# Layer 1's prototype bias as stacked half-precision parts instead of a full-precision product

## The reference

```
topw, topi = top_k(softmax(-dists / t), 2);  topw = topw / sum(topw)
out = zeros
for tslot in range(2):
    idx, wt = topi[:, tslot], topw[:, tslot:tslot + 1]
    h = einsum('nri,ni->nr', B[idx], xf)          # rank 16
    out = out + wt * (einsum('nor,nr->no', A[idx], h) + bias[idx])
x = x + tanh(g_ffn[1]) * out
```

## Time and profile before

| | us |
|---|---|
| median of 3 runs | 3636.69 (3634.04 to 3637.95) |
| profiled execution, its time | 3638.66 |
| profiled execution, its span | 3636.8 |
| PE busy, share of the span | 3096.3, 85% |
| DVE busy | 2824.3, 78% |
| ACT busy | 2012.7, 55% |
| POOL busy | 1970.1, 54% |

### The profile page before, as it was taken

How to read it: one execution, slowest core, us unless ns; L and a number is a source line. 1 busy time by engine, 2 the same in 40 slices (tenths; PEclk the granted TensorE clock), 3 DMA queues, 4 the chain that set the end, 5 groups by cost and what they waited for, 6 DMA issues and landing times. The chain is left out here.

```text
span 3636.8 us, 107677 instructions
## 1 busy us (share of the span) xinstructions
PE 3096.3 (85%) x35590; PEld 2626.8 (72%) x35590; DVE 2824.3 (78%) x6978; ACT 2012.7 (55%) x4103; POOL 1970.1 (54%) x3561
## 2 busy tenths in 40 slices
PE   4999884777777777599986999999999999999998
PEld 2666663565655656499984888888888888888886
DVE  5777775878788888656536988888888888888896
ACT  2666664777777777345533554545554555555553
POOL 0000004656566565000003888888888888888887
PEclk8999997999999999799997999999999999999999
DMA  3666562222222221211012232323232323232321
GB/s 118 264 265 246 234 254 58 74 71 64 73 71 64 73 71 53 89 48 47 23 36 87 76 99 87 100 87 100 88 99 87 100 87 100 87 100 87 100 86 52
DMA packets 352441, 364.00 MB, mean 100 GB/s; under 512 B 109953, under 2 KB 332673, under 8 KB 347137
## 3 DMA queue, kind: packets, MB, share of 16 engines
q1 hardware_dynamic: 338944, 333.23, 28.5%
q10 hardware_dynamic: 12960, 25.23, 1.9%
q0 software_dynamic: 160, 0.52, 0.1%
HBM read 213.11 MB, written 145.78 MB: 99 GB/s over the span
## 5 line engine op out<-in xcount | busy, mean ns | idle before, releaser
L365 POOL TENSOR_TENSOR a_probT_lo<-a_expT,a_probT_hi 128x512 f16<-128x512 f32 (+1 forms) x384 | 371.4, 995 | 343.2 <-ACT a_probT_hi L433 343.2
L933 POOL TENSOR_TENSOR a_pn<-a_prob,a_rsum 128x1232 f32<-128x1232 f32 x128 | 360.3, 2815 | 6.6 <-DVE a_rsum L1273 6.6
L1031 ACT ACTIVATE a_qT_hi<-banks 128x512 f16<-128x512 f32 x256 | 152.8, 597 | 360.2 <-PE banks L140 360.2
L138 PE MATMUL banks<-a_vo,a_probT_hi 128*128 128x256 f16 x1280 | 349.2, 273 | 2.7 <-DVE a_probT_lo L1246 2.6
L139 PE MATMUL banks<-a_vo,a_probT_hi 128*128 128x256 f16 x1280 | 349.2, 273 | 0.0
L140 PE MATMUL banks<-a_vo,a_probT_lo 128*128 128x256 f16 x1280 | 349.0, 273 | 0.0
L138 PE MATMUL banks<-a_xnT_hi,w_q_hi 128*128 128x256 f16 x1024 | 282.3, 276 | 4.7 <-DVE a_xnT_lo L1244 4.5
L139 PE MATMUL banks<-a_xnT_lo,w_q_hi 128*128 128x256 f16 x1024 | 282.3, 276 | 0.0
L140 PE MATMUL banks<-a_xnT_hi,w_q_lo 128*128 128x256 f16 x1024 | 282.2, 276 | 0.0
L424 ACT ACTIVATE a_expT<-banks,a_top,w_score_scale 128x512 f32<-128x512 f32 (+1 forms) x384 | 269.7, 703 | 22.6 <-PE banks L519 11.5
L1967 POOL PARTITION_ALL_REDUCE w_tops<-w_part_tops x1 | 0.4, 368 | 498.3 <-DVE w_part_tops L1994 498.3
(11 more groups left out here) (346 smaller groups left out, 12469.7 us busy)
## 6 DMA issues: line engine op xcount, KB each, us to landing
vo<-kv_vo_out SPq DMA_DIRECT2D x38, 2048.0 KB, 6.7
a_vo<-vo SPq DMA_DIRECT2D x64, 1152.0 KB, 5.8
kt<-kv_k_out ACTq DMA_DIRECT2D x9, 2560.0 KB, 14.6
a_k<-kt SPq DMA_DIRECT2D x64, 308.0 KB, 3.3
a_x<-in_x SPq DMA_DIRECT2D x64, 256.0 KB, 2.9
a_y<-in_x SPq DMA_DIRECT2D x64, 256.0 KB, 2.7
x<-a_y SPq DMA_DIRECT2D x64, 256.0 KB, 2.2
moe_raw<-in_L_ffn_w SPq DMA_DIRECT2D x16, 1024.0 KB, 7.5
```

Source lines behind the costliest of these rows:

```text
L138: nc.tensor.matmul(out, lhs[0], rhs[0], start=start, stop=False)
L365: pool.tensor_tensor(probT[b][1][0:rows, first:end, :], expT[b][0:rows, first:end, :], probT[b][0][0:rows, first:end, :], ALU.subtract).th ...
L933: pool.tensor_tensor(by_key(pn[h]), by_key(prob_of(u, h, 2)), rsum[h][:, :].unsqueeze(1).broadcast_to([P, KEYS, H]), ALU.mult).then_inc(pn ...
L1031: act.activation(out, bank[:, 0:cols].rearrange("p (c s) -> p c s", c=out.shape[1]), ACT.Copy, scale=scale)\
```

## The change

The bias product becomes a half-precision one over 96 rows: rows 0 to 31 are the high part of the weights times the high part of the table, rows 32 to 63 the high part times the table's low part, rows 64 to 95 the low part of the weights times the table's high part.

- `wsel` is written three times side by side (96 columns instead of 32).
- `wselT` is half precision on 96 rows. ACT writes all of it and raises the new `wselT_hi`; DVE then subtracts on rows 64 to 95 and raises `wselT_ready`. DVE does this between the statistics (L1366) and `prep(2)`.
- In the set-up the table is loaded three times (96 rows) without waiting for POOL, one more maximum is taken and reduced, the unit of `UP` is raised where the bias needs it, and the table is scaled, copied to half precision and, for rows 32 to 63, replaced by its remainder.

```
@@ attention_ffn_phase
-    wselT = sb("wselT", [P, P])
+    wselT = sb("wselT", [BIAS_ROWS, P], F16)            # BIAS_ROWS = 96
@@ ACT
-                    act.activation(wselT[:, :], bank[:, 0:P], ACT.Copy).then_inc(wselT_ready, 1)
+                    act.activation(wselT[:, :], bank[0:BIAS_ROWS, 0:P], ACT.Copy).then_inc(wselT_hi, 1)
@@ DVE, behind bn_stats(stats2), ahead of prep(2)
+                if live(t - 7, NT):
+                    bank, rows = full(i, ("wselT", h)), slice(2 * NPROTO, BIAS_ROWS)
+                    need(dve, wselT_hi, t - 6)
+                    nc.vector.tensor_tensor(wselT[rows, :], bank[rows, 0:P], wselT[rows, :], ALU.subtract)\
+                        .then_inc(wselT_ready, 1)
@@ DVE
-                    nc.vector.tensor_tensor(wsel[:, 0:NPROTO], pick[:, 0, :], pick[:, 1, :], ALU.add)\
+                    nc.vector.tensor_tensor(wsel[:, 0:BIAS_ROWS].rearrange("p (r n) -> p r n", r=3),
+                                            pick[:, 0, :].unsqueeze(1).broadcast_to([P, 3, NPROTO]),
+                                            pick[:, 1, :].unsqueeze(1).broadcast_to([P, 3, NPROTO]), ALU.add)\
@@ layer1_weights
-    low_bias_sb, proto_sq = sb("low_bias", [P, D]), sb("proto_sq", [P, NPROTO])
+    low_bias_sb, proto_sq = sb("low_bias", [BIAS_ROWS, D], F16), sb("proto_sq", [P, NPROTO])
-            sp.wait_ge(bias_zero, 1)
-            sp.dma_start(low_bias_sb[0:NPROTO, :], low_bias).then_inc(small_in, 16)
+            for r in range(3):
+                sp.dma_start(raw_bias[r * NPROTO:(r + 1) * NPROTO, :], low_bias).then_inc(small_in, 16)
-            pool.memset(low_bias_sb[:, :], 0.0).then_inc(bias_zero, 1)
-            pool.wait_ge(tops_part, 4)
+            pool.wait_ge(tops_part, 5)
+            dve.wait_ge(small_in, 64)
+            nc.vector.reduce_max(part_tops[0:NPROTO, 4:5], raw_bias[0:NPROTO, :], AX.X, apply_absolute_value=True)\
+                .then_inc(tops_part, 1)
-            step(nc.vector.tensor_scalar(units[:, :], units[:, :], SMALL, 1.0 / WEIGHT_TOP, ALU.max, ALU.mult))
-            nc.vector.reciprocal(inverse[:, :], units[:, :]).then_inc(inverse_ready, 1)
+            step(nc.vector.tensor_scalar(units[:, 0:4], units[:, 0:4], SMALL, 1.0 / WEIGHT_TOP, ALU.max, ALU.mult))
+            step(nc.vector.reciprocal(low_unit[:, 0:1], units[:, DOWN:DOWN + 1]))
+            step(nc.vector.scalar_tensor_tensor(out=low_unit[:, 0:1], in0=low_unit[:, 0:1], scalar=1.0 / KEY_TOP,
+                                                in1=units[:, 4:5], op0=ALU.mult, op1=ALU.mult))
+            step(nc.vector.tensor_tensor(units[:, UP:UP + 1], units[:, UP:UP + 1], low_unit[:, 0:1], ALU.max))
+            nc.vector.reciprocal(inverse[:, :], units[:, 0:4]).then_inc(inverse_ready, 1)
-            nc.vector.tensor_scalar(low_bias_sb[:, :], low_bias_sb[:, :], low_unit[:, 1:2], None, ALU.mult)
+            step(nc.vector.tensor_scalar(raw_bias[:, :], raw_bias[:, :], low_unit[0:BIAS_ROWS, 1:2], None, ALU.mult))
+            nc.vector.tensor_copy(low_bias_sb[:, :], raw_bias[:, :]).then_inc(bias_hi, 1)
+            dve.wait_ge(bias_hi, 1)
+            rows = slice(NPROTO, 2 * NPROTO)
+            nc.vector.tensor_tensor(low_bias_sb[rows, :], raw_bias[rows, :], low_bias_sb[rows, :], ALU.subtract)
```

More of the change, by code:

```diff
@@ L40 @@
 LC = LOW // P
+BIAS_ROWS = 3 * NPROTO
 E, TOPK, FF, MOE_T = 8, 2, 1024, 1024
@@ L780, in attention_ffn_phase @@
         sem("top_step"), sem("top_used"), sem("wtops_ready"), sem("picked"), sem("wsel_ready"))
-    low_ready, hw_ready, hwT_hi, hwT_ready, wselT_ready, out_ready = (
-        sem("low_ready"), sem("hw_ready"), sem("hwT_hi"), sem("hwT_ready"), sem("wselT_ready"), sem("out_ready"))
+    low_ready, hw_ready, hwT_hi, hwT_ready, wselT_hi, wselT_ready, out_ready = (
+        sem("low_ready"), sem("hw_ready"), sem("hwT_hi"), sem("hwT_ready"), sem("wselT_hi"), sem("wselT_ready"),
+        sem("out_ready"))
     def prep_uses(h, part):
@@ L2027, in layer1_weights @@
     raw_in = [sem(f"raw_in{n}") for n in range(4)]
-    small_in, bias_zero, turned, hi_done, lo_done, sq_done, sq_full, step_sem, ones_set = (
-        sem("small_in"), sem("bias_zero"), sem("turned"), sem("hi_done"), sem("lo_done"), sem("sq_done"),
+    small_in, bias_hi, turned, hi_done, lo_done, sq_done, sq_full, step_sem, ones_set = (
+        sem("small_in"), sem("bias_hi"), sem("turned"), sem("hi_done"), sem("lo_done"), sem("sq_done"),
         sem("sq_full"), sem("step"), sem("ones_set"))
@@ L2038, in layer1_weights @@
         part_tops, units, inverse, low_unit = (
-            tmp("part_tops", [P, 4]), tmp("units", [P, 4]), tmp("inverse", [P, 4]), tmp("low_unit", [P, 2]))
+            tmp("part_tops", [P, 5]), tmp("units", [P, 5]), tmp("inverse", [P, 4]), tmp("low_unit", [P, 2]))
+        raw_bias = tmp("raw_bias", [BIAS_ROWS, D])
         block = inner.enter_context(nc.Block())
@@ L2120, in _ @@
                     .then_inc(tops_part, 1)
+            dve.wait_ge(small_in, 64)
+            nc.vector.reduce_max(part_tops[0:NPROTO, 4:5], raw_bias[0:NPROTO, :], AX.X, apply_absolute_value=True)\
+                .then_inc(tops_part, 1)
             dve.wait_ge(tops_ready, 1)
-            step = Steps(dve, step_sem, 0, 9)
-            step(nc.vector.tensor_scalar(units[:, :], units[:, :], SMALL, 1.0 / WEIGHT_TOP, ALU.max, ALU.mult))
-            nc.vector.reciprocal(inverse[:, :], units[:, :]).then_inc(inverse_ready, 1)
+            step = Steps(dve, step_sem, 0, 13)
+            step(nc.vector.tensor_scalar(units[:, 0:4], units[:, 0:4], SMALL, 1.0 / WEIGHT_TOP, ALU.max, ALU.mult))
[4 more added lines that the diff above has]
+            nc.vector.reciprocal(inverse[:, :], units[:, 0:4]).then_inc(inverse_ready, 1)
             step(nc.vector.tensor_tensor(score_scale[:, :], units[:, Q:Q + 1], const["key_unit"][:, 1:2], ALU.mult))
@@ L2134, in _ @@
             nc.vector.tensor_copy(proto_sq[:, :], psum[:, 5 * BANK:5 * BANK + NPROTO])
-            dve.wait_ge(small_in, 32)
-            nc.vector.tensor_scalar(low_bias_sb[:, :], low_bias_sb[:, :], low_unit[:, 1:2], None, ALU.mult)
+            step(nc.vector.tensor_scalar(raw_bias[:, :], raw_bias[:, :], low_unit[0:BIAS_ROWS, 1:2], None, ALU.mult))
[3 more added lines that the diff above has]
+            nc.vector.tensor_tensor(low_bias_sb[rows, :], raw_bias[rows, :], low_bias_sb[rows, :], ALU.subtract)
             step(nc.vector.tensor_scalar(neg[:, :], mit[:, :], -1.0, None, ALU.mult))
```

## The result

The median after the change is 3690.15 us (3688.15 to 3693.48) against 3636.69: ratio 1.015, 95% interval 1.0126 to 1.0173. That is +53.5 us where +37 was forecast, and 0.15 us beyond the upper end of the range. The profiled execution's span grew from 3636.8 to 3691.7, by 54.9.

The account below looks back on a forecast made before the run. Bound: a loop of waits through PE, ACT and DVE. Per turn +0.87 stall, -0.32 product, +0.06 `wsel` = +0.61; 58 turns +35.4, set-up +1.8, total +37.2: 3674 us, range 3662 to 3690, low end stretched to 3655.

Parts of the forecast that it names:

- The loop of waits: Layer 1: PE's h = 0 output product through h = 1, ACT's `qT_hi`, DVE to `dots`, back to PE; 25.39 us a turn.
- DVE's additions: Subtraction (0.29) and wider `wsel` (0.06) on DVE: hidden by its waits, except `wsel` of h = 1, 0.06 a turn.
- The five signs: Profile after: PE's subtraction wait 0.9, bias product 0.11, DVE's q1 wait 0.7 or more, q3 wait and PE share lower.
- The sixth: Sign in the profile after: one turn of the loop through PE, ACT and DVE takes 26.0 us.
- the stall: PE before the output product of h = 0, waiting for DVE's subtraction: starts at 2815.84 instead of 2814.97, 0.87 lost a turn.
- Start of the subtraction: DVE, h = 0: subtraction starts 0.41 behind the statistics' start, the middle of 0.35 (overlapping) and 0.47 (not overlapping).
- Length: DVE's subtraction of 128 columns out of PSUM: 0.29 us, with ends 0.24 and 0.42.
- Hop from DVE's end to PE's product: From the subtraction's end on DVE to PE's first product: 0.14 us, taken from the same hop behind `dots`.
- The fixed part of the set-up: Before the loop: extra maximum 0.40, three dependent DVE steps 0.57, copy and subtraction 0.8; together +1.8, ends 1 and 3.
- The drain: At the end of the kernel: the cheaper product and the later release cancel, 0.
- Rival 1: DVE doesn't overlap subtraction and statistics: start at 0.47, PE loses 0.93 a turn, +40.7, 3677 us; chance 0.29.
- Rivals 2, 3 and 4: In order: PE not made to wait, 3623 (0.08); DVE becomes bound, 3681 (0.07); even, within 7 us of 3637 (0.06).

Follow-up runs that it names:

- e4: Kernel before (full-precision bias product, old set-up) with only the subtraction added, into a tile nothing reads, and the product's wait moved to it: 3702.8 us, ratio 1.0184.
- e1: Changed kernel, with PE waiting for the subtraction only in front of the bias product, behind the twelve half-precision products: 3630.3 us, ratio 0.9984.
- e6: Changed kernel with DVE's subtraction moved up two instructions, right behind `dots`, PE's wait in its old place: 3651.3 us, ratio 1.0041.
- e3: Changed kernel with the three blocks of 32 rows reordered, so that the subtraction works on rows 0 to 31: 3678.4 us, ratio 1.0116.
- e2: Changed kernel with the wait for the subtraction put last of PE's three waits in front of the output product: 3679.8 us, ratio 1.0120.
- e5: Changed kernel without the subtraction, ACT raising `wselT_ready` as before, the low part of the weights left out: 3633.0 us, ratio 0.9990.
- e7: Changed kernel with the wait for the subtraction last of three and the subtraction on rows 0 to 31: 3672.2 us, ratio 1.0095.
- e9: Changed kernel with PE's wait only in front of the bias product and the subtraction on rows 0 to 31: 3630.9 us, ratio 0.9985.
- e8: Changed kernel with PE's wait in front of the bias product, the subtraction right behind `dots` and on rows 0 to 31: 3634.5 us, ratio 0.9992.
- e10: e9 plus three products of a zero tile in half h = 1, in front of the bias product: 3624.3 us, ratio 0.9967.

## Why the prediction was off

**The mechanism held.** The loop of waits (PE, ACT, DVE, `dots`) was read rightly: the product counts once of two (e4), h = 1 is beside it, DVE's additions are covered, and the subtraction's place behind the statistics is the price (e1, e6). The five signs named for it came: a wait of 0.9, the product's 0.11 to its successor, DVE's wait for q1 kept (0.98 at 2823.01), that for q3 down from 0.81 to 0.51, PE's busy share down. The sixth, a turn of 26.0 us, came as 26.18.

**The step that failed is a term's size: the stall, 0.87 forecast, 1.06 in the turn shown, and in it above all the hop from DVE to PE.** Its parts:

- Start of the subtraction behind the statistics: 0.41 taken, 0.45 to 0.46 measured. The middle was a hedge between two kinds of neighbour. e3 shows the one that the rows decide: 0.34 on rows 0 to 31.
- Length: 0.29 and 0.29.
- Hop from DVE's end to PE's product: 0.14 taken from `dots`. Measured are 0.26 as the median in h = 0 (0.25 to the weight load, the product 0.01 later) and 0.29 in the turn shown. The prediction took every wait of PE to be released as that for `dots` is. Behind that one the weight load is the next instruction; here a second instruction of the sequencer stood between, and e2 takes its 0.13 away.

With 0.79 instead of 0.61 in some 59 turns, that is 11 us of the 17 that were missing, 7 of them by the hop.

The turn alone didn't leave the range. Its upper bound had the same stall, 1.06, and +0.87 a turn. But it came to 1.06 by a length of 0.42 that was not met, with the hop still at 0.14, so that it covered the hop was luck. The sum as it stands, with 58 x 0.79 + 1.8, gives 3684. The time came out past 3690 by this together with what follows: the set-up, 3.8 instead of 1.8, and the jumps, 3.6 where the sum had nothing.

**The fixed part of the set-up** is as forecast, 1.8: the last maximum to the reduction +0.32, the reduction to ACT's first split +0.59, `q_lo`'s start to the next phase +0.88. But the load of `raw_q`, which both kernels wait for, landed later. The kernel before, then the changed one:

```profile
1902.24 2.29 DVE L2119 TENSOR_REDUCE w_part_tops<-w_raw_q 128x1 f32<-128x2048 f32 x1 [10.25 <-DMA w_raw_q<-in_L_xattn_Wq]
```

```profile
1905.48 2.29 DVE L2128 TENSOR_REDUCE w_part_tops<-w_raw_q 128x1 f32<-128x2048 f32 x1 [14.09 <-DMA w_raw_q<-in_L_xattn_Wq]
```

From the phase's first instruction to this maximum it takes 11.4 us in the changed kernel, 7.5 in the kernel before, 10.0 in e4, whose set-up is the old one, and 8.2 to 12.6 in the others. So it varies with either set-up; whether the three loads add to it isn't settled. The load came 3.8 later. Against that stand 0.7, since the wait for `raw_a` is gone, 0.6 by which the phase began earlier, and 0.5 less behind it. With the fixed 1.8 that makes the +3.8 at the first `dots`.

**The jumps were left out, +3.6.** The program jumps back 13 times. PE's first transposes after one of them, kernel before and then changed kernel, and the clock in the same place (window, length, busy, clock):

```profile
3273.58 0.53 PEld L1151 LDWEIGHTS banks<-ident,a_pn 128*128 128x128 f32 x5 [1.92 <-issue]
```

```profile
3273.50:3274.70 1.20, 1.11 (x13) 0.95 (x15) 0.04 (x1) 0.42 (x1) 1.13 (x2) 1.00 0.13 43
```

```profile
3319.16 1.57 PEld L1153 LDWEIGHTS banks<-ident,a_pn 128*128 128x128 f32 x8 [2.75 <-issue]
```

```profile
3319.00:3321.00 2.00, 1.83 (x8) 1.57 (x8) 0.36 (x1) 0.60 (x1) 1.84 (x6) 0.50 0.46 138
```

PE stands idle 2.75 us instead of 1.92, and comes back with a granted clock of 0.50, which is 1.2 GHz: eight transposes' weights take 1.57 us. In the kernel before the idle time at the 13 jumps is 1.8 to 2.4 and the clock is 1.00 after each. In the changed one it is 2.5 to 3.0, and 4 of 13 come back low; those four turns take 29.2 to 29.6, the others 28.7 to 29.2. By their means, 29.41 and 28.86, the low clock costs 0.55 in each of the four, 2.2 of the 3.6. Why PE idles longer there isn't settled. That the semaphore holds PE back was my theory A in e5, and it fell. e4, with the old product, has 2.2 to 2.8 and six low clocks, so the product's length is not all of it either.

**The drain** was put at 0 and came to some +2 in the last four sequences; e5, e7 and e9 show 0 to -1 there, e6 and e8 +2, so I read nothing from it.

**Rival 1** (held neighbours, 3677) was right in its mechanism: the start was 0.45 to 0.46 and the next instruction didn't overlap. It missed the hop as the forecast did. Rivals 2, 3 and 4 are excluded by the new wait, by DVE's kept waits and by the turn.

## What to carry to other kernels

When a producer is moved to another engine, price the place in that engine's order, not its length: 0.29 us of subtraction cost 1.05 a turn behind two long instructions, 0.2 right behind `dots`, and nothing once its consumer waited for it where it needed it. Put each wait in front of the one instruction that needs it, and where it needs several, the one that comes up last behind the others in the program: that was worth 0.12 us a turn here (e2). A saving counts only where it lies on the loop of waits: the second of two equal products brought nothing.

## What I had not expected

- The order of three waits in front of one product is worth 0.13 us each time. Where a second instruction of the sequencer stands behind the wait that ends last, the weight load comes 0.24 behind the subtraction, and 0.11 where none does (the changed kernel and e2).
- More PE work made the kernel faster. With three idle products of 0.11 in one half the median is 6.6 us lower (e10 against e9), of which the traces give 3 to 4 us to the loop.
- PE can lose its clock in a gap at a loop's jump. In the changed kernel it came back at a granted clock of 0.50 from one of 2.52 us (weight load at 2243.85), and in e8 at 1.00 from one of 3.51.
